# The block-diagonal operand of the G product: filled by eight small DMAs a group, instead of by a GpSimd product each tile

## What is computed

```python
x = x0                                   # (512, 40, 16), gathered from 40 tables
outputs = []
for k in (k0, k1, k2):                   # (128,40,40), (128,128,40), (128,128,40)
    x = jnp.einsum('bhd,bmd,ohm->bod', x, x0, k)
    outputs.append(jnp.sum(x, axis=-1))
z = jnp.concatenate(outputs, axis=1)
h = jnp.concatenate([z, dense_ctx], axis=1)
h = jnp.maximum(h @ W_top1 + b_top1, 0.0)
h = jnp.maximum(h @ W_top2 + b_top2, 0.0)
y = h @ W_top3
```

## Time and profile before

| | |
|---|---|
| median of 3 runs | 703.82 us (703.36 to 705.27) |
| the profiled execution | 706.33 us, span 704.4 us |
| PE busy | 651.3 us, 92% |
| VectorE (DVE) busy | 619.2 us, 88% |
| ScalarE (ACT) busy | 554.1 us, 79% |
| GpSimd (POOL) busy | 321.0 us, 46% |
| granted TensorE clock | 0.995 of full speed |

### The profile page before, as it was taken

How to read it: one execution, slowest core, us unless ns; L and a number is a source line. 1 busy time by engine, 2 the same in 40 slices (tenths; PEclk the granted TensorE clock), 3 DMA queues, 4 the chain that set the end, 5 groups by cost and what they waited for, 6 DMA issues and landing times.

```text
span 704.4 us, 11705 instructions
## 1 busy us (share of the span) xinstructions
PE 651.3 (92%) x2502; PEld 463.7 (66%) x2502; DVE 619.2 (88%) x1355; ACT 554.1 (79%) x1950; POOL 321.0 (46%) x250
## 2 busy tenths in 40 slices
PE   0389999999989999999999999999999999999998
PEld 0157776776767777777667777777777767765573
DVE  2559999999999999999899999999999999988390
ACT  2158888888888988888788888898888898889383
POOL 6645564636364655556463647465545611110000
PEclk9989999999999999999999999999999999999999
DMA  6431212121312122221213130212222122400000
GB/s 212 115 88 49 76 46 80 45 80 33 92 21 56 53 52 72 50 74 46 80 34 91 31 89 22 62 48 51 74 49 75 45 79 65 174 3 0 30 2 0
DMA packets 56671, 43.00 MB, mean 61 GB/s; under 512 B 37007, under 2 KB 40335, under 8 KB 56352
## 3 DMA queue, kind: packets, MB, share of 16 engines
q1 hardware_dynamic: 51488, 41.08, 19.7%
q0 software_dynamic: 5120, 1.32, 2.3%
HBM read 40.41 MB, written 1.97 MB: 60 GB/s over the span
## 4 chain that ended last, share of the span: by engine, by line
PE 76%; DVE 14%; issue 5%; DMA 2%; POOL 1%; DVEq 1%; SPq 0%; ACT 0%
PE Y L572 17%; PE Y L574 16%; PE Y L573 16%; PE X L539 14%; DVE sums L487 4%; PE GB L546 4%; DVE sums L436 2%; DVE sums L431 2%; DVE sums L449 2%; PE X L610 1%; POOL x0g L288 1%; DMA pairs<-scratch 1%; DVE x1lo L420 1%; PE X L612 1%; PE X L611 1%
## 5 line engine op out<-in xcount | busy, mean ns | idle before, releaser
L372 ACT ACTIVATE sums<-Y,xtok 128x128 f32<-128x128 f32 x1792 | 493.4, 395 | 91.1 <-PE Y L574 91.0
L572 PE MATMUL Y<-k1lo,x1hi 128*128 128x512 f32 x640 | 315.5, 493 | 20.3 <-DVE sums L487 17.1
L574 PE MATMUL Y<-k1hi,x1lo 128*128 128x512 f32 x640 | 253.5, 396 | 0.0
L573 PE MATMUL Y<-k1hi,x1hi 128*128 128x512 f32 x640 | 252.8, 395 | 0.0
L487 DVE SCALAR_TENSOR_TENSOR sums<-Y,xtok,sums 128x128 f32<-128x128 f32 x768 | 229.4, 341 | 24.2 <-PE Y L574 21.9
L317 POOL TENSOR_TENSOR diag<-xtok,mask 128x320 f32<-128x320 f32 x64 | 103.9, 1624 | 267.2 <-PE GB L546 267.0
L288 POOL DMA_INDIRECT x0g<-in_table,rows_now x160 | 199.2, 1245 | 42.2 <-issue 38.6
L572 PEld LDWEIGHTS Y<-k1lo,x1hi 128*128 128x128 f32 x640 | 120.6, 188 | 82.2 <-DVE sums L487 27.8
L573 PEld LDWEIGHTS Y<-k1hi,x1hi 128*128 128x128 f32 x640 | 121.1, 189 | 50.6 <-issue 25.3
L539 PE MATMUL X<-pairs,w 120*128 120x512 f32 x224 | 116.9, 604 | 29.8 <-DVE pairs L416 29.8
L574 PEld LDWEIGHTS Y<-k1hi,x1lo 128*128 128x128 f32 x640 | 120.7, 189 | 29.2
(11 more groups left out here) (64 smaller groups left out, 249.3 us busy)
## 6 DMA issues: line engine op xcount, KB each, us to landing
pairs<-scratch SPq DMA_DIRECT2D x112, 240.0 KB
A<-scratch SPq DMA_DIRECT2D x16, 240.0 KB
k1raw<-in_k SPq DMA_DIRECT2D x1, 2560.0 KB, 10.6
x0g<-in_table,rows_now POOLq DMA_INDIRECT x160, 3.2
k2s<-in_k SPq DMA_DIRECT2D x1, 2560.0 KB, 9.1
scratch<-x0g SPq DMA_DIRECT2D x96, 20.0 KB, 1.7
pairs<-in_w SPq DMA_DIRECT2D x3, 256.0 KB, 3.0
w2s<-in_w SPq DMA_DIRECT2D x1, 512.0 KB, 4.0
```

The lines of the kernel that those rows point to most:

```text
L372: ins = nc.scalar.activation(sums[tile % 2][:, k * O:(k + 1) * O], Y[(NCH * tile + c) % YB][:, i * O:(i + 1) * O], ACT.Copy, scale=xtok[sl ...
L572: nc.tensor.matmul(y, hi[:, tok], k1lo[:, cols], start=True, stop=False)
L573: nc.tensor.matmul(y, hi[:, tok], k1hi[:, cols], start=False, stop=False)
L574: nc.tensor.matmul(y, lo[:, tok], k1hi[:, cols], start=False, stop=True).then_inc(s_y, 1)
```

## The change

GpSimd's product per tile is gone. `diag` becomes one buffer for a whole group, with the example b ahead of m; its zeros and its mask column are written once, in the prologue, and for each group eight DMAs of SyncE (`blocks`), one per example of a tile, put the 16 rows of `xtok` of that example into their block, for the four tiles at once. SyncE issues them behind the fourth fill of `pairs`, once the last G product of the group before is done. GpSimd's body is only row numbers and gathers, ten in a row; `take_rows` has an added instruction, `settled`. ScalarE's copy of G reads the G product's bank in the new order.

```diff
-        diag = [sb(f"diag{i}", [P, MH, SB]) for i in range(2)]
+        diag = sb("diag", [P, TPG, SB, MH])
+            def blocks(u, slot):
+                g = u * GPB + slot
+                sp.wait_ge(s_xtok, g + 1)
+                sp.wait_ge(s_G, TPG * g + 2)
+                for b in range(SB):
+                    rows = slice(b * D, (b + 1) * D)
+                    sp.dma_start(diag[rows, :, b, 0:M], xtok[slot % 2][rows, :, :]).then_inc(s_diag, 16)
...
                 for c in range(NC0):
                     n, buf, _ = chunk(u, slot, c)
+                    if slot >= 0 and c == NR:
+                        blocks(u, slot)
...
+                if last:
+                    blocks(u, GPB - 1)
...
                 pool.wait_ge(s_rows, g + 1)
+                nc.gpsimd.tensor_tensor(settled[:, :], base[:, 0:1], base[:, 0:1], ALU.add)
...
             def body(u, last):
-                for tile in range(GPB * TPG):
-                    slot, j = tile // TPG, tile % TPG
-                    T = u * (GPB * TPG) + tile
-                    gathers = not last or slot < GPB - 2
-                    if gathers and j == 0:
-                        pool.wait_ge(s_prod, NC0 * (u * GPB + slot + 1))
-                        take_rows(u * GPB + slot + 2, slot % 2)
-                    pool.wait_ge(s_xtok, u * GPB + slot + 1)
-                    pool.wait_ge(s_G, T + 1)
-                    nc.gpsimd.tensor_tensor(
-                        diag[tile % 2][:, 0:M, :],
-                        xtok[slot % 2][:, j, :].unsqueeze(2).to_broadcast([P, M, SB]),
-                        mask[:, :].unsqueeze(1).to_broadcast([P, M, SB]), ALU.mult).then_inc(s_diag, 1)
-                    if gathers and j < GATHER_TILES:
-                        gather(slot % 2, range(-(-GF * j // GATHER_TILES), -(-GF * (j + 1) // GATHER_TILES)))
+                for slot in range(GPB - 2 * last):
+                    pool.wait_ge(s_prod, NC0 * (u * GPB + slot + 1))
+                    take_rows(u * GPB + slot + 2, slot % 2)
+                    gather(slot % 2, range(GF))
...
                     G[:, :, bass.ds((T + 1) * SB, SB)],
-                    GB[:, 0:MH * SB].rearrange("p (m b) -> p m b", b=SB), ACT.Copy).then_inc(s_Gout, 1)
+                    GB[:, 0:MH * SB].rearrange("p (b m) -> p m b", b=SB), ACT.Copy).then_inc(s_Gout, 1)
...
-            def make_G(T, buf):
+            def make_G(T, buf, g, j):
                 pe.wait_ge(s_merge, MERGE * (T + 3))
-                pe.wait_ge(s_diag, T + 2)
+                pe.wait_ge(s_diag, 16 * SB * (g + 1) + 1)
                 pe.wait_ge(s_Gout, T + 2)
-                nc.tensor.matmul(GB[:, 0:MH * SB], x2[buf][:, :], diag[buf][:, :, :].rearrange(
-                    "p m b -> p (m b)"), start=True, stop=True).then_inc(s_G, 1)
+                nc.tensor.matmul(GB[:, 0:MH * SB], x2[buf][:, :], diag[:, j, :, :].rearrange(
+                    "p b m -> p (b m)"), start=True, stop=True).then_inc(s_G, 1)
```

More of the change, by code:

```diff
@@ L68 @@
 X1_LAG = {"x1hi": 1, "x1lo": 2, "z0": 3}
-GATHER_TILES = 3
 MERGE_AT = (0, 1, 2, 3)
@@ L133, in build @@
         base = sb("base", [P, GF], i32)
+        settled = sb("settled", [P, 1], i32)
         rows_now = [sb(f"rows_now{i}", [P, GF], i32) for i in range(2)]
@@ L295, in _ @@
                 gather(g, range(GF))
-            for i in range(2):
-                nc.gpsimd.memset(diag[i][:, :, :], 0.0).then_inc(s_dzero, 1)
-            pool.wait_ge(s_dzero, 2)
+            nc.gpsimd.memset(diag[:, :, :, :], 0.0).then_inc(s_dzero, 1)
+            pool.wait_ge(s_dzero, 1)
             pool.wait_ge(s_const, 32)
-            for i in range(2):
-                nc.gpsimd.tensor_copy(diag[i][:, M, :], mask[:, :]).then_inc(s_dones, 1)
-            pool.wait_ge(s_dones, 2)
+            for j in range(TPG):
+                nc.gpsimd.tensor_copy(diag[:, j, :, M], mask[:, :]).then_inc(s_dones, 1)
             nc.gpsimd.memset(credit[:, 0:1], 0.0).then_inc(s_G, 1)
+            pool.wait_ge(s_dones, TPG)
             nc.gpsimd.memset(credit[:, 1:2], 0.0).then_inc(s_diag, 1)
             def body(u, last):
-                for tile in range(GPB * TPG):
-                    slot, j = tile // TPG, tile % TPG
-                    T = u * (GPB * TPG) + tile
-                    gathers = not last or slot < GPB - 2
-                    if gathers and j == 0:
-                        pool.wait_ge(s_prod, NC0 * (u * GPB + slot + 1))
-                        take_rows(u * GPB + slot + 2, slot % 2)
-                    pool.wait_ge(s_xtok, u * GPB + slot + 1)
-                    pool.wait_ge(s_G, T + 1)
-                    nc.gpsimd.tensor_tensor(
-                        diag[tile % 2][:, 0:M, :],
-                        xtok[slot % 2][:, j, :].unsqueeze(2).to_broadcast([P, M, SB]),
-                        mask[:, :].unsqueeze(1).to_broadcast([P, M, SB]), ALU.mult).then_inc(s_diag, 1)
-                    if gathers and j < GATHER_TILES:
-                        gather(slot % 2, range(-(-GF * j // GATHER_TILES), -(-GF * (j + 1) // GATHER_TILES)))
+                for slot in range(GPB - 2 * last):
+                    pool.wait_ge(s_prod, NC0 * (u * GPB + slot + 1))
+                    take_rows(u * GPB + slot + 2, slot % 2)
+                    gather(slot % 2, range(GF))
             over_groups(pool, body)
@@ L334, in prep @@
                         act.wait_ge(s_chain, STT * (TPG * (g - 1) + 1))
-                        act.wait_ge(s_diag, TPG * (g - 1) + 1)
+                        act.wait_ge(s_diag, 16 * SB * (g - 1) + 1)
                     nc.scalar.activation(xtok[par][:, :, :], TR[:, 0:TPG * PR].rearrange(
@@ L577, in body @@
                         if c == G_AT:
-                            make_G(T - 1, (tile - 1) % 2)
+                            make_G(T - 1, (tile - 1) % 2, u * GPB + (tile - 1) // TPG, (tile - 1) % TPG)
             over_groups(pe, body)
@@ L596, in _ @@
                 if i == H1 // P // 2:
-                    make_G(NTILES - 1, (NTILES - 1) % 2)
+                    make_G(NTILES - 1, (NTILES - 1) % 2, NG - 1, TPG - 1)
                 nc.tensor.matmul(Y[i][:, :], w1s[0][:, i * P:(i + 1) * P], z0[:, :], start=False, stop=False)
```

## The result

The changed kernel takes **754.89 us** (median of 6 runs, 753.18 to 759.94), the kernel before beside it 703.59 us (6 runs). The ratio is 1.0724, 95% interval 1.07 to 1.0748: slower by 7%, where 697.9 us was forecast. The profiled execution took 753.93 us, its span is 752.1 us.

A forecast was written before the change was run, and what follows sets the result against it. Mostly TensorE bounds the kernel, with VectorE setting the end in tiles without L0 products. A faster `early` gives -6.1 us, `settled` +0.2, so -5.9 from 703.82: 697.9 us, range 695.0 to 702.5.

The forecast's parts named there:

- the one on GpSimd's queue: Gathers no longer stand between products; SyncE's vanished wait for them hid nothing; only `settled` before the first gather adds 0.2 us.
- Rival 3: Ten gathers in a row beside VectorE's additions each hold VectorE 0.42 us, 2.1 us a group: 730 us; chance 0.03.
- Rival 4: Diagonal blocks land 3.3 us late at 1.34 us a DMA, PE waits 15 or 16 times: 748 us; chance 0.04.
- 6.1 us less: `early`'s second addition loses its wait for GpSimd's product; on the chain 10 x 0.42 plus 6 x 0.32 us.
- the last tiles' stalls: PE's stalls in group 15's last three tiles, 0.77 us before, each shorten by 0.32 us.
- The loop's jump: Before groups 4 and 8 the next addition waits 2.8 us for VectorE's sequencer whatever L436 takes, so no gain there.
- An issue of a block DMA: On SyncE's queue, 0.46 us each, eight a group 3.7 us, inside 9.1 us before the G product needing them: cost zero.
- the 0.1 us that I took: Added time of ScalarE's copy of G reading PSUM with a step of 41; bound 0.46 us; off the chain.
- rival 2: ScalarE's copy doubles or more and ends the tile, or chunk 6's fill comes 0.4 us late: 703.8 us; chance 0.07.
- the thin cover of chunk 6: Next `scratch` writes go directly behind chunk 6's `pairs` fill, sharing DMA engines 1.2 us of 1.5 spare; 0.3 left, cost zero.
- `k2s` and the MLP's weights: At the end, loaded behind group 15's blocks, all landed by 644.4, 3 us before the MLP's first products: cost zero.

The follow-up runs named there:

- later start: Changed kernel with ten gathers in a row, started at the G where the first part started before the change, about 11 us later: 739.67 us, ratio 1.047.
- early start: The changed kernel's own start of its ten gathers, as soon as the seven L0 operands of the group two before are made: 754.89 us, ratio 1.0724.
- sixteen additions between: Changed kernel, its own gather start and no added wait, eight one-column GpSimd additions behind the fourth and the seventh gather: 703.82 us, ratio 0.9978.
- the two cut kernels: Changed kernel with each group's gathers in parts behind waits for G: 4, 3, 3 (700.52 us, ratio 0.993) and 3, 3, 2, 2 (700.34 us, 0.9916).

## Why the prediction was wrong

**The step that failed** is the one on GpSimd's queue. It saw that the ten gathers would now stand in a row, named SyncE's wait for them as the only thing that their old spacing touched, and said that it "hid nothing". It costed the run at nothing. The runs put 39 us (later start: 739.7 against 700.5) to 51 us (early start: 754.9 against 703.8 with sixteen additions between) in its place, and the trace shows the wait that was missing from the sum: ScalarE and VectorE wait for TensorE's late counts of finished chunks, 4.10 and 4.17 us in the two groups shown. Beside chunks the trace of before had no more than four gathers in a row. It has two runs of ten, but in the prologue (3.7 to 16.1 and 17.4 to 29.8 us), where TensorE makes no chunk that they could delay. For ten beside chunks, which no row shows, the step gave neither bound. It should have: the run became two and a half times as long.

**Rival 3** had the right objects, ten gathers in a row, and the wrong mechanism. It let each gather hold VectorE, 0.42 us a time, and gave 730 us. VectorE's additions beside gathers have their usual length (L433 1.214 us, 1.215 before; L438 1.225), so no gather held it. The VectorE instruction inside a gather in the earlier trace rows had said so. It is the other way round, VectorE holds gathers: of the 130 gathers after the first 60 us of the changed kernel 37 take over 1.1 us, where one alone takes 0.94. Each of them begins while VectorE works on two operands in SBUF, and ends 0.81 to 0.91 us after that instruction; the gather of 1.93 us above is held by an L433 from 337.12 to 338.33. The rule of the Trainium skill (SBUF — State Buffer, "Who interferes with whom") on which the rival rested shows for gathers in this order only. What waits is ScalarE and VectorE, for hand-overs from TensorE. (Gathers stand in 14 groups, where the rival has 15.) **Rival 4** came near the time, 748, by luck, with a mechanism that did not occur: the block DMAs took 0.59 us of the queue (min, median, max below), eight of them 5.2 us, landed 1.8 us later, and TensorE never waits for `diag`.

```profile
L246 SPq DMA_DIRECT2D diag<-xtok x128: 585/595/1167, 57.5 to 674.9; - x128
...
DMA to landing us min/median/max: 1.8/1.8/2.7
```

**The rest of the sum held.** Of "6.1 us less" by a faster `early`, step by step: L438 takes 1.225 us (1.23 forecast); the last tiles' stalls are 0.43 for 0.77 us. In the kernel with parts of 3, 3, 2 and 2, TensorE's stall in the middle groups' tile without L0 products is 0.56 where it was 1.01:

```profile
311.16 0.50 PE L577 MATMUL Y<-k1lo,x1hi 128*128 128x512 f32 x1 [0.56 <-DVE sums L492]
```

Over that kernel TensorE's wait for VectorE falls by 5.7 us (17.1 to 11.4). The loop's jump eats the gain of groups 4 and 8, as forecast: the addition behind it starts 3.1 us after L436 did before, and 3.2 us after the shorter L441 did here (194.76 to 197.88, 192.56 to 195.77). An issue of a block DMA is 0.59 us, not 0.46: eight take 5.2 instead of 3.7 us, inside the 9.1 us that there were. ScalarE's copy of G costs 0.468 us for 0.461; of the 0.1 us that I took, 0.007 came, so rival 2 has nothing to stand on. The fills of `pairs` make VectorE wait 10.1 us in the kernel with parts of 4, 3, 3, and 9.6 before: the thin cover of chunk 6 held. `k2s` and the MLP's weights are in none of TensorE's waits. The forecast of 697.9 us is 0.9916 of 703.82; the two cut kernels measured 0.993 (0.9903 to 0.9958) and 0.9916 (0.9882 to 0.9951), and hold it in their intervals.

**What stays open.** The record of the semaphore shows that TensorE's counts come late and in bunches, while hand-overs to TensorE stay at 0.05 us. How gathers bring that about isn't settled: whether TensorE sends the counts late or they are held on their way, no run separates. Nor is it settled why the early start costs 15 us more than the later one (754.9 and 739.7), why ten in a row cost the kernel before only 28 us, whether time or number counts, how long a run may be and how long the pause behind it must be. Parts of five with a real pause between them would be the next kernel to try.

## What to carry to other kernels

An instruction that is slow and in nobody's way can still do a job by where it stands: here a product of GpSimd, replaced for its 0.42 us, was also what broke up a run of gathers. When an experiment sets pauses, read in its trace whether they came: two kernels here had almost none where they were meant to. When a change lets an engine's work go closer together than any row of the trace shows, treat that as a new operation with an unknown price in both directions. If indexed gathers must come in numbers, the arrangements that cost nothing measurable here are parts of at most four with some 1.7 us or more of waiting or other GpSimd work between them, and pairs with 0.8 us or more. With the early start such pauses were worth 51 us.

## What the runs showed of the hardware

- During a run of ten gathers by index that GpSimd issues, from some 9 us into it, TensorE's increments of a semaphore come late (by 2.1 and 4.2 us in the group shown) and then in bunches (four within 0.16 us), though its matmuls start on time. 47 increments of the changed kernel's trace follow another within 0.2 us, 27 with parts of 5 and 5, 45 with 7 and 3, 1 with 4, 3 and 3, none in the kernel before and none with plain transfers. Hand-overs from ScalarE and VectorE to TensorE took 0.05 us all the while.
- From the same start, over 14 groups, ten in a row cost 39 us, with a break of 0.6 us behind the seventh 26 us, with one of 0.6 us behind the fifth 9.5 us (739.7, 726.9 and 710.0 against 700.5 us). Waits and GpSimd's small additions both serve as pauses.
- Twenty plain transfers from the same queue, 10.3 us without a pause, did nothing of the kind. A gather takes GpSimd at least 0.90 us for 64 rows and 0.94 for 128, a plain transfer 0.53 (5.29 for ten).
- A VectorE instruction with two SBUF operands holds a gather that starts inside it, up to 1.93 us where one alone takes 0.94, and not a plain transfer (0.54 at most of 76 that started so, with ten plain ones). A gather does not hold such a VectorE instruction (L438: 1.225 us).
- A stall of some 2 us was followed by more than 2 us at half TensorE's clock (0.50 from 342 to 344), so that stalls cost about twice their length over this kernel: 22.5 us of waits and, as an estimate, 23.6 us of clock.
